# Expert stage of a token tower: when the transposed z is moved, when the routing weights are prepared, and where one copy stands

## What is computed

```python
h = h + ffn(layernorm(h))             # 4096 tokens of 192 values
z = einsum('nd,sdr->nsr', x, P)       # 8 sub-spaces s, 16 values r each
scores = einsum('nsr,smr->nsm', z, C) # 64 experts m in each sub-space
topv, topi = top_k(scores, 4); w = softmax(topv)
hid = gelu(z @ W1[s, m] + b1)         # 32 hidden values, for the 4 chosen m
comb[s] = sum over chosen m of w * (hid @ W2[s, m] + b2)
out = gelu(comb @ G1 + g1b) @ G2 + g2b
```

## Time and profile before

| | us |
|---|---|
| median of 3 runs | 2925.73 |
| lowest and highest run | 2924.49, 2930.23 |
| the profiled execution's own time | 2926.53 |
| its span, first to last instruction | 2924.8 |
| mean granted TensorE clock, share of full | 0.925 |
| TensorE (matmul) busy | 2440.8 (83%) |
| VectorE busy | 1894.8 (65%) |
| ScalarE busy | 1199.3 (41%) |
| GpSimd busy | 1151.3 (39%) |

### The profile page before, as it was taken

One profiled execution on the slowest core, in us unless ns is written; L12 is line 12 of the kernel. 1 busy time (PEld: TensorE's weight loads), 2 busy tenths in 40 slices (PEclk: granted clock), 3 DMA queues, 4 the chain that ended last, 5 costly groups with the idle time before them and its releaser, 6 DMA issues. The chain is left out here.

```text
span 2924.8 us, 42167 instructions
## 1 busy us (share of the span) xinstructions
PE 2440.8 (83%) x16000; PEld 1233.9 (42%) x16000; DVE 1894.8 (65%) x3874; ACT 1199.3 (41%) x1617; POOL 1151.3 (39%) x781
## 2 busy tenths in 40 slices
PE   3556999999999999999999996048787877888788
PEld 1223555565555556555565553022322222232222
DVE  5865565565655656565565754158687876878787
ACT  3421333333333333333333332036565655666666
POOL 5000475666757566575756654021111111111010
PEclk9778999999999999999999998559899998999999
DMA  1002000000010000000000003710101011010100
GB/s 45 11 22 54 7 1 9 1 9 9 1 30 1 9 1 9 9 1 9 1 2 1 3 1 12 70 36 1 24 1 24 1 24 24 1 24 1 24 6 6
DMA packets 78698, 38.51 MB, mean 13 GB/s; under 512 B 62936, under 2 KB 71192, under 8 KB 77848
## 3 DMA queue, kind: packets, MB, share of 16 engines
q1 hardware_dynamic: 76320, 30.98, 6.1%
q10 hardware_dynamic: 640, 1.69, 0.5%
q0 software_dynamic: 1536, 3.15, 0.4%
HBM read 21.93 MB, written 10.49 MB: 11 GB/s over the span
## 5 line engine op out<-in xcount | busy, mean ns | idle before, releaser
L588 POOL TENSOR_TENSOR acc<-acc,pT 128x1024 f32<-128x1024 f32 (+3 forms) x412 | 829.7, 2014 | 242.1 <-ACT pT L907 208.8
L1622 DVE TENSOR_TENSOR hw<-hid,banks 128x512 f32<-128x512 f32 x1024 | 666.8, 679 | 196.6 <-PE banks L1368 177.7
L907 ACT ACTIVATE pT<-banks 128x1024 f32<-128x1024 f32 x480 | 405.7, 896 | 832.0 <-PE banks L661 778.4
L787 DVE TENSOR_REDUCE part<-banks 128x2 f32<-128x1024 f32 (+3 forms) x432 | 437.9, 1043 | 312.8 <-PE banks L637 311.1
L1495 ACT ACTIVATE hid<-banks 128x1024 f32<-128x1024 f32 x512 | 497.7, 1022 | 275.1 <-PE banks L1358 232.7
L1368 PE MATMUL banks<-wT,select 64*128 64x512 f16 x1024 | 369.7, 409 | 60.9 <-DVE hw L1622 43.1
L677 PE MATMUL banks<-pT,v 128*64 128x512 f32 (+3 forms) x1920 | 405.2, 543 | 1.5 <-POOL pT L576 1.5
L1358 PE MATMUL banks<-zst,w1c 50*128 50x512 f32 x1024 | 340.0, 566 | 11.2 <-ACT hid L1495 9.8
L1376 PE MATMUL banks<-hw,w 128*32 128x512 f32 x2048 | 293.9, 648 | 7.1 <-DVE hw L1622 7.1
L1368 PEld LDWEIGHTS banks<-wT,select 64*128 64x128 f16 x1024 | 96.5, 96 | 454.3 <-DVE hw L1622 376.6
L637 PE MATMUL banks<-kh,qh 64*128 64x512 f32 (+1 forms) x960 | 192.1, 395 | 13.1 <-ACT pT L907 5.6
(11 more groups left out here) (183 smaller groups left out, 2934.0 us busy)
## 6 DMA issues: line engine op xcount, KB each, us to landing
zst<-z_scratch SPq DMA_DIRECT2D x48, 128.0 KB, 4.3
z_scratch<-zp SPq DMA_DIRECT2D x8, 512.0 KB, 3.5
out_h<-o SPq DMA_DIRECT2D x8, 384.0 KB, 2.7
xT_scratch<-xs_hi SPq DMA_DIRECT2D x4, 512.0 KB, 2.7
xt_hi<-xT_scratch SPq DMA_DIRECT2D x2, 1024.0 KB, 5.6
w1c<-raw1p ACTq DMA_DIRECT2D x12, 132.0 KB, 4.7
w1c<-raw1p SPq DMA_DIRECT2D x12, 132.0 KB, 4.1
wo<-in_L_attn_W_O SPq DMA_DIRECT2D x12, 96.0 KB, 1.9
```

What stands on the lines that cost most here:

```text
L588: pool.tensor_tensor(acc[:, G % 2, :, off:CH], acc[:, G % 2, :, off:CH], pT[:, slot, :, 0:w], ALU.add).then_inc(summed, 1)
L787: last = dve.tensor_reduce(to[:, :, c:c + 1], both[:, :, 0:whole], AX.X, ALU.max)
L907: act.activation(pT[:, J % PSLOTS, :, 0:CH - off], both[:, :, 0:CH - off], ACT.Exp, scale=E ** -0.5)\
L1622: dve.tensor_tensor(hw[:, n % 2, q, :], hid[:, n % 2, q, :], ring_bank(("w", g, n, q)), ALU.mult).then_inc(mixed, 1)
```

## The change

Six edits, all in `stage_experts`:

1. `bounce_z(g + 2)` is put ahead of the store of group g's output; before, `bounce_z(g + 1)` stood ahead of it. The items of z move back by one or two steps (`Z_AT`, `SUMS_AT`, `VARIANCE_AT`, `REFINE_AT`), and `split_z` from (15, 3) to (18, 0).
2. GpSimd's order becomes divide 0, low 0, divide 1, low 1.
3. VectorE's keeps, casts and TensorE's transposes of weights move forward.
4. The 32 marks are spread as before, one behind each mix from step 16, but two behind each mix of steps 18 and 19, so they end with step 21 and not 23.
5. ScalarE's `take_mixture` goes ahead of the second gelu of step 1 of the next group.
6. The two parts of `bias_down` (TensorE, 12 matmuls each) go from steps 18 and 22 to 19 and 21.

```diff
-        Z_AT = {11: (0,), 12: (1,), 13: (2,)}
-        PREP_AT = {5: (3, 4), 7: (5, 6), 24: (7,), 25: (8,), 27: (9,), 28: (10,)}
+        Z_AT = {13: (0,), 14: (1,), 15: (2,)}
+        PREP_AT = {5: (3, 4), 7: (5, 6), 23: (7,), 24: (8,), 26: (9,), 27: (10,)}
         OUT_AT = {1: (0,), 2: (1,), 3: (2,)}
         EXP_AT = 17
-        BIAS_AT = (18, 22)
+        BIAS_AT = (19, 21)
-        BEST_FROM, MARK_FROM = 8, 16
-        KEEP_AT = {(20, 2): 0, (21, 2): 1, (24, 0): 2, (24, 2): 3}
-        HIGH_AT = {(23, 1): 0, (26, 1): 1}
+        BEST_FROM = 8
+        MARKS = [(n, q) for n in range(16, 22) for q in range(NQ) for _ in range(2 if n in (18, 19) else 1)]
+        KEEP_AT = {(20, 1): 0, (20, 3): 1, (21, 1): 2, (22, 1): 3}
+        HIGH_AT = {(22, 0): 0, (24, 0): 1}
         DEN_AT, RECIPROCALS_AT = (16, 0), (20, 0)
-        SUMS_AT, VARIANCE_AT, REFINE_AT, SPLIT_AT = (5, 0), (7, 0), (9, 0), (15, 3)
+        SUMS_AT, VARIANCE_AT, REFINE_AT, SPLIT_AT = (6, 0), (8, 0), (10, 0), (18, 0)
...
             for g in range(NG):
-                if 1 <= g < NG - 1:
-                    bounce_z(g + 1, (g + 1) % 2)
+                if g < NG - 2:
+                    bounce_z(g + 2, g % 2)
                 sp.wait_ge(out_ready, g + 1)
...
-                divide(g, 0)
-                divide(g, 1)
-                low_weights(g, 0)
-                low_weights(g, 1)
+                for part in range(2):
+                    divide(g, part)
+                    low_weights(g, part)
...
+                    if n == 0 and g:
+                        take_mixture(g - 1)
                     if next1[0] < NG:
                         gelu(*next1, 1)
-                    if n == 0 and g:
-                        take_mixture(g - 1)
...
-                if MARK_FROM <= n < MARK_FROM + 8:
-                    mark(g, (n - MARK_FROM) * NQ + q)
+                for i in range(GT * S):
+                    if MARKS[i] == (n, q):
+                        mark(g, i)
```

## The result

The changed kernel takes 2836.73 us (median of 4 runs, 2836.0 to 2837.2) against 2925.11 us of the kernel before, measured with it. The ratio is 0.9695, with a 95% interval of 0.9678 to 0.9712: faster by 88 us. Forecast were 2829.5 us and 96 us less. The profiled execution took 2836.9 us, its span is 2835.2.

A forecast was written before the change was run, and what follows sets the result against it. Steps were taken as bound by TensorE (2.55 us), by VectorE (steps 16 to 24), or by waits for z and low weights. Savings 59.4 + 6.7 + 30.1 = 96.2 us gave 2829.5 us, range 2805 to 2856.

The forecast's parts named there:

- The weights and marks: Steps 12 to 31: new places for weights work and marks save 6.7 - 1.9 - 0.5 us a group, 30.1 us in seven groups.
- the 2.0 us a group in steps 12 to 15: Steps 12 to 15 lose `make_z` and `split_z`, taking 12.5 us where 14.53 were taken.
- The 3.5 us put down for the clock: Allowance of 0.5 us a group, seven groups, for TensorE's clock falling where VectorE keeps it waiting through steps 20 to 22.
- The held keeps: Keeps 2 and 3, steps 21 and 22, stand until GpSimd ends: 0.3 and 1.55 us lost, together 1.9 a group.
- The first rival, keeps not held: Keeps 2 and 3 are not delayed by GpSimd: 13 us more saved, 2816 us, or 2807 with the clock given back; 15%.
- The load of z: Wait before step 6's scores goes, 52.0 us, plus 5.6 for clock and 1.8 for `sums` and `variance`: 59.4 us.
- the price of 0.75 us for `sums` and `variance`: Moved to steps 6 and 8, ahead of the mix TensorE's spread awaits, they cost 0.75 us each, bounds 0 and 1.1.
- the middle, 0.8: Step 6 at full clock gains between 0 and 1.7 us in each of 7 groups; 0.8 taken, 5.6 us in all.
- The mixture copy: Step 1: ScalarE's copy ahead of the gelu saves 0.96 us, bounds 0.4 to 0.96, in seven groups: 6.7 us.
- The rival "half clock": TensorE falls to 1.2 GHz in steps 20 to 22, reaching 23 to 25: 24 us lost, 2853 us; 10%.

The follow-up runs named there:

- e3: The kernel before with only the bounce of group g + 2 put ahead of the store of group g's output on SyncE's queue; 2866.36 us, ratio 0.9798.
- e12: The kernel before with two edits, the bounce ahead of the output's store and the mixture copy ahead of the gelu; 2865.25 us, ratio 0.9791.
- e10: The changed kernel with all of z's items back at the places of the kernel before; bounce, copy and weights as changed; 2863.84 us, ratio 0.9744.
- the keeps clear: The changed kernel with keep 2 moved to (21, 2) and keep 3 to (23, 0), outside GpSimd's work; 2818.61 us, ratio 0.9630.
- e1: The changed kernel with sums, variance and refine back in steps 5, 7 and 9; 2830.28 us, ratio 0.9667.
- Two small edits together: The changed kernel with sums and variance one quarter later, keep 2 at (21, 2) and keep 3 at (23, 0); 2792.87 us, ratio 0.9541.

## Why the prediction was right, and where it was off

**The weights and marks** (forecast 30.1, measured 31.1 us) came out term by term. Forecast and measured for group 1: steps 16 and 17 together 7.8 and 7.80; 18 and 19 8.8 and 8.80; step 20 5.1 and 5.10; step 21 4.2 and 4.24 with the keep held; step 22 5.15 and 5.17; step 23 2.55 and 2.54; steps 24 and 25 6.8 and 6.86. These steps are VectorE's own work in a row, and such work can be summed from durations. One size was off: the 2.0 us a group in steps 12 to 15 were counted in seven groups, but group 6 prepares no z and gained nothing there. The 3.5 us put down for the clock were spent, nearly all in group 4: steps 12 to 31 take 73.1 us there against 69.8 in its neighbours, with steps 23 and 24 at half clock. Step 23:

```profile
2490.33:2494.22 3.89, 2.47 (x5) 0.50 0.02 6
```

**The held keeps** were right in mechanism and size: 1.01 and 2.24 us against 1.0 and 2.2. The row that carried this was of another instruction in another stage. The first rival, keeps not held, is refuted. Against the price of 1.9 us a group, removing the delays gave 2.0 in group 2, and 2.5 in the mean with the clock.

**The load of z** was right: the wait of 52.0 us has gone, and the store is issued in step 18. By itself the bounce gave 58.8 us in steps 5 to 11, where 52.0 + 5.6 = 57.6 were forecast. The change as a whole gave only 46.9 there, where 59.4 were forecast, and those 12.5 us are the miss. Five of the kernels form a chain that adds one part of the change at a time, and it shows where they went. Groups 0 to 6, us:

| kernel | steps 5 to 11 | of them at 1.2 GHz | steps 12 to 31 |
|---|---|---|---|
| before | 234.2 | 78.5 | 523.3 |
| with the bounce (e3) | 175.4 | 17.1 | 525.5 |
| and the mixture copy (e12) | 182.8 | 41.0 | 524.1 |
| and the weights' part (e10) | 187.7 | 58.0 | 505.4 |
| and z's items: the changed kernel | 187.3 | 58.0 | 492.2 |

The copy took back 7.4 us and the weights' part 4.9, both as half clock in steps whose instructions they do not touch. Each row is one execution, so the 4.9 are less certain than the 58.8. The move of z's items took nothing: at full clock steps 5 to 10 are 0.3 us a group shorter by it (21.8 us in group 1 of the bounce alone, 21.5 in group 1 with the keeps clear), the gain that was forecast. So the step of the prediction that was off is not the price of 0.75 us for `sums` and `variance`, which is what steps 6 and 8 show at full clock (4.82 against 4.10, 5.09 against 4.31). It is that the clock was priced in step 6 alone, as a gain, "the middle, 0.8", and that the other parts of the change were taken to leave it alone.

Small gains stand against the miss: 1.0 us in the weights, 0.5 in the other steps, 2.2 since the stage begins at 1953.8 and not 1955.9, and 2.2 between the last mix and the end of the span (13.1 us before, 10.9 after). 12.5 - 5.9 = 6.6 us, which is 96.2 less the 89.6 by which the span fell. The last two, 4.4 us, had no term in the sum: the number came closer by luck.

**The mixture copy** was right as a step (0.96 us in seven groups) and wrong as a gain: with the kernel before, and with the bounce alone, the total did not move. The prediction counted a step's gain as the kernel's.

**The rival "half clock"** had the right mechanism and only in part the right place. It was set at steps 23 to 25; it came there in two groups, and in steps 6 to 9 in all seven.

The Trainium skill has a passage that bears on this ("TensorE: Matmul & The Clock Gate", section "A second HAM failure mode: psum-queue depth-cycling"): in a kernel that cycles through PSUM banks, short idle times of TensorE between groups of matmuls make its clock swing between half and full. The traces agree only in part. The idle pieces of 0.78 and 0.54 us stand ahead of products of 1.93 us in the changed kernel, but pieces of 0.79 and 0.54 us stand ahead of products of 1.07 with the keeps clear.

**What stays open:** why the same steps with the same instructions ran at full clock in one kernel and at half in another. Steps 5 to 8 of the bounce alone and of e1 are an example (4.08 against 5.94 us for step 6), step 6 of the changed kernel and of the keeps clear is another (6.18 against 4.82), and within one run step 6 of the bounce alone took 6.28 us in group 2. The runs show which edits shift it, not the rule.

## What to carry to other kernels

Look at what a DMA is queued behind before looking at the DMA: the load of z was late because its store stood behind an output that was not ready, and moving two lines brought two thirds of the gain. Where GpSimd and VectorE work on the same tiles, set the VectorE instructions with two SBUF inputs outside of GpSimd's work, and small reductions behind the operation for which another engine waits, not ahead of it. A gain in a single step is a gain of the kernel only if TensorE's clock in the steps after it stays as it was; so compare the sum over a whole period, and the granted clock beside it.

## What the runs showed of the hardware

- A VectorE instruction that reads two SBUF tiles and is issued while GpSimd works stands until GpSimd ends, less 0.12 to 0.14 us: 0.68 us became 1.01 and 2.24, and 1.22 became 2.64. The keeps have a scalar and two tensors, and are held like the sum of two tensors. A cast was held once too, ahead of the first group of the kernel before: 0.69 us became 2.59 with 2.04 left of GpSimd's low half. Mixes, which read one of their tiles from PSUM, and marks were not held under the same GpSimd instructions.
- Step 6 of the bounce alone took 4.08 us at full clock and 6.28 at a granted clock of 0.56; step 8 took 4.31 at full clock and, in the copy alone, 6.45 at 0.50 (1.2 GHz). Over the stage the mean granted clock ranged from 0.89 to 0.97 between kernels with the same instructions in another order; shortening one step by 0.96 us was enough to move it from 0.91 to 0.89.
- Two small edits together brought 44 us where each brought 18 to 19: TensorE's time at half clock over the stage fell from 129.7 us to 107.3 and 93.8 with one of them, and to 54.6 with both.
- DMA traffic beside a step at the floor cost it nothing: with the output's store, at a DMA share of 0.47, step 5 took 2.55 us.
